# Edge network of a graph kernel: eight buffers for gathered source rows instead of four, loops of two iterations a turn, and weighted one-hots made in one vector instruction each

## What is computed

```python
h = relu(layernorm(x))                              # [12500, 96]
# edge network (the stage that is changed)
e = concat([h[src], edge_attr_32])                  # [400000, 128]
messages = gelu(e @ mW1 + mb1) @ mW2 + mb2
gates = sigmoid(gelu(e @ gW1 + gb1) @ gW2 + gb2)    # [400000, 1]
agg = segment_sum(messages * gates, dst, 12500)
update = gelu(concat([h, agg]) @ uW1 + ub1) @ uW2 + ub2
x = x + layernorm(h + update) * ln_g + ln_b
# two convolutions
h = relu(layernorm(x)); y = h
for W, b, Wr, br in layers:                         # 2 layers
    norm = dinv[src] * edge_weight * dinv[dst]      # self loops added
    conv = segment_sum(norm * (y @ W)[src], dst) + b
    g = sigmoid(y @ Wr + br)
    y = relu((1 - g) * y + g * conv)
out = x + y
```

## Time and profile before

| | |
|---|---|
| median of 3 runs | 11252.27 us (11244.29 to 11253.65) |
| the profiled execution | 11244.56 us, span 11242.6 us |
| edge pass, plain iterations (without building) | 160 to 680 us |
| edge pass, building iterations (175) | 680 to 5405 us |
| update stage | 5405 to 5650 us |
| the two convolution passes | 5650 to 11242 us |
| PE, PEld busy over the span | 8235.0 us (73%), 5614.5 us (50%) |
| DVE, ACT, POOL busy over the span | 5197.6 us (46%), 2896.6 us (26%), 6709.2 us (60%) |
| mean granted TensorE clock | 0.848 |

### The profile page before, as it was taken

How to read it: one execution, slowest core, us unless ns; L and a number is a source line. 1 busy time by engine, 2 the same in 40 slices (tenths; PEclk the granted TensorE clock), 3 DMA queues, 4 the chain that set the end, 5 groups by cost and what they waited for, 6 DMA issues and landing times.

```text
span 11242.6 us, 161615 instructions
## 1 busy us (share of the span) xinstructions
PE 8235.0 (73%) x40104; PEld 5614.5 (50%) x40104; DVE 5197.6 (46%) x17514; ACT 2896.6 (26%) x6502; POOL 6709.2 (60%) x6696
## 2 busy tenths in 40 slices
PE   5567666666767676667748888888875888888886
PEld 4334444444444444444435556555553555555554
DVE  5566666666666676666612222222231222222223
ACT  4345555555555555555300000000000000000000
POOL 4666565565566565656456666666645666666663
PEclk7678888888888888888768888888876988888887
DMA  4346566565566665656346666666664666666666
GB/s 151 81 132 175 166 175 172 167 174 168 171 174 175 172 176 172 172 168 174 128 144 230 229 236 237 228 232 233 228 205 152 232 225 235 231 233 232 232 229 204
DMA packets 1329034, 2149.88 MB, mean 191 GB/s; under 512 B 306427, under 2 KB 1079948, under 8 KB 1328700
## 3 DMA queue, kind: packets, MB, share of 16 engines
q10 hardware_dynamic: 142400, 986.64, 24.3%
q1 hardware_dynamic: 925996, 684.95, 20.7%
q0 software_dynamic: 260560, 477.49, 15.9%
HBM read 1587.45 MB, written 560.99 MB: 191 GB/s over the span
## 4 chain that ended last, share of the span: by engine, by line
PE 56%; issue 15%; another core or an unknown queue 15%; ACT 7%; DVE 3%; DMA 2%; POOL 1%; DVEq 1%; ACTq 1%; SPq 0%; POOLq 0%
PE bd L1159 30%; PE bd L1055 11%; PE sg L1146 6%; ACT blocks L1286 3%; PE pb L1044 3%; PE sg L1074 2%; PE pa L1044 2%; ACT hid L1265 2%; ACT msg L1278 1%; ACT gate_t L1271 1%; PE bd L1108 1%; PE bd L1171 0%; PE bd L1167 0%; DMA out_nodes<-s_c 0%
## 5 line engine op out<-in xcount | busy, mean ns | idle before, releaser
L909 POOL DMA_INDIRECT hid<-src_table,src_ids x3127 | 3188.8, 1020 | 2068.0 <-ACT msg L1278 1080.4
L1159 PE MATMUL bd<-ring,table_sb 128*96 128x280 f32 x13720 | 3580.3, 420 | 254.6 <-issue 145.1
L1159 PEld LDWEIGHTS bd<-ring,table_sb 128*96 128x96 f32 x13720 | 2332.5, 172 | 1408.7 <-issue 545.7
L1055 PE MATMUL bd<-one_hot_dst,one_hot_src 128*128 128x343 bf16 x8400 | 1751.2, 353 | 1449.9 <-ACT blocks L1286 1135.8
L953 POOL DMA_INDIRECT hid<-conv_table,hid x1724 | 1660.3, 963 | 1058.5 <-issue 512.4
L1055 PEld LDWEIGHTS bd<-one_hot_dst,one_hot_src 128*128 128x128 bf16 x8400 | 841.3, 108 | 2251.8 <-issue 1787.4
L1286 ACT ACTIVATE blocks<-bd 128x686 f32<-128x686 f32 x1400 | 1116.8, 798 | 2255.3 <-remote 1489.7
L953 POOL DMA_INDIRECT feat_in<-conv_table,hid x1152 | 1121.3, 973 | 618.3 <-issue 334.0
L1871 DVE TENSOR_TENSOR acc<-acc,sg 96x64 f32 x434 | 94.6, 218 | 2527.3 <-remote 1188.3
L1391 ACT ACTIVATE side_out<-bd,side_flag 96x280 f32<-96x280 f32 x70 | 34.3, 490 | 4022.5 <-issue 2294.1
L1885 DVE TENSOR_TENSOR acc<-acc,side_out 96x7 f32 x2800 | 469.6, 168 | 1256.2 <-issue 933.5
(11 more groups left out here) (226 smaller groups left out, 6957.8 us busy)
## 6 DMA issues: line engine op xcount, KB each, us to landing
ring<-adjacency ACTq DMA_DIRECT2D x980, 980.0 KB
adjacency<-blocks SPq DMA_DIRECT2D x700, 686.0 KB
attr<-in_attr SPq DMA_DIRECT2D x392, 128.0 KB
hid<-src_table,src_ids POOLq DMA_INDIRECT x3127
hid<-conv_table,hid POOLq DMA_INDIRECT x1724
feat_in<-conv_table,hid POOLq DMA_INDIRECT x1152
conv_table<-table_sb SPq DMA_DIRECT2D x28, 336.0 KB, 4.7
feat_half<-feat_keep SPq DMA_DIRECT2D x56, 168.0 KB
```

The source lines that it names most:

```text
L909: pool.indirect_dma_start(out=hid[s][:, t, :], out_offset=None, in_=src_rows, in_offset=bass.IndirectOffsetOnAxis(ap=src_ids[s // 2][:, j: ...
L1055: op = nc.tensor.matmul(bd[:, 512 * h:512 * h + HALF_Z], y[:, 1 + k, :], z[:, Z_PAD * h:Z_PAD * h + HALF_Z], start=(k == 0), stop=(k == 2))
L1159: op = nc.tensor.matmul(side_ps, table_sb[:, D * k:D * (k + 1)], ring[slot][:, :, QUAD_FANS * b:QUAD_FANS * (b + 1)], start=(k == 0), stop ...
```

## The change

It does three things.

**Eight buffers.** `hid` gets four more buffers, so that the quads of odd iterations have their own. They lie in memory that is free during the edge pass (`feat_space[0]`, `feat_space[1]`, `buf_h[1]`, `buf_b[1]`). Each has its own semaphore for landed gathers. POOL now starts quad s of iteration n when quad s of iteration n-2 has been weighed. The index lists keep their two buffers, and SP's program keeps its order: the list of a group is loaded after the gathers of that group of iteration n-1 have landed, and behind the store of four built tiles.

**Two iterations a turn.** Since a buffer's name must stand in the code, the loops over building iterations do two iterations a turn; the first two building iterations stand alone. ACT's early loads for the update stage that used the new buffers move behind its edge pass.

**One-hots.** The unweighted one-hot is gone. Each of the three weighted ones is made by one instruction that compares and multiplies (`is_equal`, then `mult`). That takes eight instructions of DVE out of each building iteration (L1601, 1400 in all) together with the wait between them and L1608, and leaves 24 instructions that now do two operations.

```diff
-            y_s = [sb_in(edges_phase, f"one_hot_src{i}", [P, 4, P], BF16) for i in range(SLOTS)]
+            y_s = [sb_in(edges_phase, f"one_hot_src{i}", [P, 3, P], BF16) for i in range(SLOTS)]
...
-        hid = [hid_all[:, QUAD * H2 * s:QUAD * H2 * (s + 1)].rearrange("p (t f) -> p t f", f=H2)
-               for s in range(QUADS_PER_ITER)]
+        hid_own = [hid_all[:, QUAD * H2 * s:QUAD * H2 * (s + 1)] for s in range(QUADS_PER_ITER)]
+        hid_own += [t[:, 0:QUAD * H2] for t in (feat_space[0], feat_space[1], buf_h[1], buf_b[1])]
+        hid = [t.rearrange("p (t f) -> p t f", f=H2) for t in hid_own]
...
-                with eng.Fori(alone, OCTETS - 1) as o:
-                    it = eng.snap(o + BUILD_FROM)
-                    iteration(it, n0 + it, False, False, (o, eng.snap(o0 + o)))
+                with eng.Fori(0, (OCTETS - 1 - alone) // 2) as v:
+                    for w in range(2):
+                        first = BUILD_FROM + alone + w
+                        it, turn = eng.snap(v * 2 + first), eng.snap(v + first // 2)
+                        o = eng.snap(v * 2 + (alone + w))
+                        iteration((it, turn, first % 2), n0 + it, False, False, (o, eng.snap(o0 + o)))
...
+        def slot_of(at, s):
+
+            it, turn, parity = at
+            return QUADS_PER_ITER * parity + s
...
-                            wait_apart(sp, s_gath[s], gathered(it - 1, QUAD, QUAD_SPARED[s]))
+                            slot = slot_of(before(at), s)
+                            wait_apart(sp, s_gath[slot], gathered(before(at)[1], slot))
                     sp.dma_start(src_ids[b][:, :], chunk(io["src"], it * 2 + b)).then_inc(s_ids[b], 16)
...
-                        wait_apart(pool, s_gated, QUADS_PER_ITER * (n - 1) + s + 1)
+                        wait_apart(pool, s_gated, QUADS_PER_ITER * (n - 2) + (s + 1 + GATED_CREDIT))
...
-                            out=hid[s][:, t, :], out_offset=None, in_=src_rows,
+                            out=hid[slot][:, t, :], out_offset=None, in_=src_rows,
...
-                for t in (t0, t0 + 1):
-                    v.tensor_scalar(y_s[t % SLOTS][:, 0, :], iota_lo[:, :], side_now[:, 0, t:t + 1], None,
-                                    ALU.is_equal).then_inc(s_one, 1)
-                for t in (t0, t0 + 1):
                     y, z = y_s[t % SLOTS], z_s[t % SLOTS]
                     v.tensor_scalar(z[:, :], iota_z[:, :], side_now[:, 4, t:t + 1], None, ALU.is_equal)
-                    dve.wait_ge(s_one, nb * OCTET + (t + 1))
                     for k in range(3):
-                        op = v.tensor_scalar(y[:, 1 + k, :], y[:, 0, :], side_now[:, 1 + k, t:t + 1], None, ALU.mult)
+                        op = v.tensor_scalar(y[:, k, :], iota_lo[:, :], side_now[:, 0, t:t + 1],
+                                             side_now[:, 1 + k, t:t + 1], ALU.is_equal, ALU.mult)
                     op.then_inc(s_yz, 1)
```

114 lines of the change are left out of this document (65 added, 49 removed).

## The result

| | before | after |
|---|---|---|
| median | 11248.6 us (4 runs) | 11995.9 us (4 runs, 11936.4 to 12042.1) |
| ratio | | 1.0646, 95% interval 1.0608 to 1.0684 |
| the profiled execution | 11244.6 us | 11951.6 us, span 11948.5 us |
| first to last block copy (175 iterations) | 674.3 to 5405.5 us | 714.0 to 6126.8 us |
| mean granted clock | 0.848 | 0.819 |

I had predicted 11450 us, and at most 11870. Slower was right; the size is 747 us instead of 200.

The account below looks back on a forecast made before the run. No engine full; a chain of waits sets the pace, with PE's results seen late during POOL's gathers. 11244.6 + 315 (buffers) - 120 (one-hots) + 4 (loads) = 11443.6, with 7.7 to the median 11450 us; range 10780 to 11870.

Parts of the forecast that it names:

- the reading that engines learn late of PE's results: Building iterations: while POOL gathers without pause, PE's results are seen only after the run; ACT waits 8.6 us an iteration.
- the 1000 us of POOL's waits: Building iterations: the most that more buffers could remove, 5.7 us of POOL's buffer waits in each of 175.
- the next limit: Building iterations: two index lists, loaded behind stores that wait for ACT's copies, limit POOL's lead to about six quads.
- its signs: POOL's pauses end with `src_ids`, SP waits for copies, ACT's remote waits stay at 8 us or grow, runs of 16 appear.
- The first rival: Building iterations: POOL's waits go and nothing replaces them, 21.4 to 22.5 us each, about 10350 us; chance 0.14.
- the buffers', +315 us: Building iterations: eight buffers bring no gain from POOL's side, 28.9 us each, +1.8 us; between 0 and +560 us.
- Its upper bound: Building iterations: 16 gathers on one list pause, 21.4 + 8.9 = 30.3 us an iteration.
- The pause for a list: POOL's pause in building: late results 1.44, copy 0.85, store issue 1.01, list 4.8, start about 0.8; together 8.9 us.
- The lower end: Building iterations: lists come in time and POOL's pauses stay as they are, 27.1 us an iteration.
- The last rival: Building iterations: each run held up fully, pause over 8.9 us for four quads; over 31 us, 12000 us; chance 0.05.
- The one-hots: DVE in building iterations: eight fewer instructions, two fifths of 1.76 us counted, -120 us, between 0 and -308; rows stay 258 ns.
- The update stage's loads: Start of the update stage: a DMA from ACT comes before PE's first product, 3 to 5 us once, +4 us.

Follow-up runs that it names:

- before_rest_again: Kernel before with only a small POOL power operation before each quad: 11258 us, ratio 1.0009 with late results; first run, before_rest, without them 10313 us, 1.1221.
- rest_one: lists_ahead plus a small POOL power operation before each quad, as a pause: 11274 us, ratio 0.9751 with late results; run again without them 10281 us, 1.1185.
- rest_two: lists_ahead plus a small POOL power operation before each second quad, after eight gathers: 11394 us, ratio 0.9851.
- pairs: lists_ahead, but POOL waits for two quads at once and starts eight gathers together: 9016 us, ratio 0.9821, on a chip without late results.
- the plain loads: Kernel before with ordinary DMAs of the same size from a fixed place instead of gathers: ratio 0.9438 (8663 us), again 0.8342 (9644 us).
- one_hots_alone: Kernel before with the new one-instruction one-hots and nothing else: 11533 us, ratio 1.0027.
- lists_ahead: Changed kernel with four index-list buffers, each list loaded an iteration earlier: 11530 us, ratio 1.0030.
- lists_old_hots: Eight buffers and four index lists loaded ahead as in lists_ahead, but one-hots made as before: 11595 us, ratio 1.0027.
- buffers_alone: Changed kernel with the one-hots made as before: 12146 us, ratio 1.0545.

## Why the prediction was wrong in size

**Right**: the reading that engines learn late of PE's results while POOL gathers without a pause. I had it as an inference. The rests show it: after every four gathers they take ACT's "remote" waits from 1268.1 to 121.7 us (before_rest_again) and to 226.9 (rest_one), after every eight they leave them at 1221.5 (rest_two). From it followed that eight buffers would not give the 1000 us of POOL's waits, and that was so: 1.0030 with the lists ahead. Right too was the next limit, with its signs: POOL's waits end mostly with `src_ids`, SP waits for copies alone, remote waits grow, more runs of 16 appear. The first rival (10350 us) is false on such a chip. On a chip without late results pairs reaches 20.2 us an iteration, as the rival said for POOL, yet gains only 1.8% on the kernel before, which takes 9184 us there and has no profile from that chip.

**Too strong**: that engines learn of the results when the run of gathers has ended. The copy of 3017.79 above starts with three gathers of the run still to come. Of the 270 copies with a "remote" wait in 1000 to 5000 us, 75, with 493 of the 1548 us, start when POOL has gathered for 3.5 us without a pause and goes on; in the kernel before it is 90 of 322, with 259 of the 1268 us. A run's end lets most results through, not all wait for it.

**The term that failed is the buffers', +315 us.** Its upper bound was 30.3 us an iteration and I took 28.9, "somewhat over the middle". Measured were 31.0, with the one-hots in it: +3.9 us instead of +1.8, 682 us instead of 315. The parts:

- The pause for a list: I had 8.9 us once an iteration, measured are 8.3 (131 waits in 128.9 iterations), and 11.19 in the one shown: 2.8 until the copy where I had 1.44, 2.0 for copy and store (1.86), 1.4 for the list's issue (nothing), 5.0 until POOL starts (5.6). In sum my pieces were about right.
- POOL's waits for messages: the bound put them at nothing, and 2.2 us an iteration are left.
- Gathers and the gaps between them: 20.5 us instead of 21.4.

So a list's pause came in nearly every iteration in full, and taking some half of it was the mistake: 1.4 of the 2.1 us an iteration that 28.9 us lacks. The other 0.7 us, some 120 us in all, the bound itself lacks, since it had no waits for messages; with the plain iterations below and the median, 44 us above the profiled execution and not 7.7, that puts the time above 11870 us. The lower end, "the lists come in time", needed copies in time, and by my own reading runs of gathers make copies late. It was no bound of the same mechanism but its denial, which was already counted as a rival.

The last rival, "much slower", had the time nearly right (over 31 us, 12000 us) at a chance of 0.05. Its single pause longer than 8.9 us is in the mean two waits, 8.3 us for lists and 2.2 us for messages.

**The one-hots**, -120 us, bounds 0 to -308, are the second step that failed. Measured: no gain; alone they cost 0.27%, some 30 us. By the means a row takes 322 ns, not 258; since DVE's instructions overlap a little, the busy times say better what is saved. Before, 259.8 + 683.0 us in 147.5 iterations are 6.39 us; after, 809.0/128.9 are 6.28 us. So 0.11 us of DVE's time were saved instead of 1.76: a second operation costs nearly what the dropped instructions gave back. I had ruled out a loss without a row that says so. The Trainium skill ("VectorE: DVE Perf Modes", Mode 4x_2P) has the second operation on compute slices of its own. That it would cost no time here was my conclusion, and this trace disagrees with that: 64 ns more for each of these instructions of 128 columns with two scalars. In which mode they ran no run shows.

**The plain iterations** were left out of the sum, as having no stores. They grew by 40 us in all: 24.6 to 26.1 us each (480 us for 294 gathers). Copies don't hold SP there, and still POOL now waits for lists, 75.0 us in 160 to 640 us. In SP's program the list also stands behind the load of the group before (L691), which waits for PE's attribute product, and that result comes late too. SP's waits for it with an unnamed end are 22.0 us before (L664, 160 to 640 us), and after:

```profile
SPq L691 <- remote: 147.9, 10, 21.3
```

So lists come late without any store too, and more lead is not free there either.

**The update stage's loads**: +4 us estimated; PE's first product waits 3.70 us for them, where it had waited 1.04 us, for the block copy. Yet what follows the last copy is 15 us shorter in all; where that is saved was not followed up:

```profile
6130.47 1.81 PE L1122 MATMUL pb<-feat_in,upd_top 96*96 96x448 f32 x2 [3.70 <-DMA feat_in<-feat_src]
```

**The rule of the Trainium skill** that PE and ACT wait on nobody ("SBUF — State Buffer", Who interferes with whom) was weighed against the copy of 3032.90. On chips where results come late the rows stay against it as far as it is taken to cover PE's signals; on the others the trace agrees (214.3 us of waits in pairs, all ended by PE). It speaks of memory ports, and no run here places the delay in one.

## What to carry to other kernels

Before giving a producer more buffers, list every input that it needs to start and see which of them stands in a queue behind the slow consumer: here the index list stood behind a store, and more lead only moved POOL's waits to the place where one wait costs most. A lead pays once; it raises the rate only if the producer is the limit. If waits end when another engine pauses, measure that effect alone (here with rests), see what else the experiment changes (the plain loads took the runs away too), and run it on more than one chip. And when a bound has been built from measured pieces, don't halve it toward an end that contradicts the mechanism it is built on.

## What was not expected of the hardware

- Results of PE come late during gathers in four of the six sessions (three chips of five). The kernel before takes 9184 and 9194 us on two chips, and 22 to 26% more in the other sessions. What makes the difference isn't known. It is not confined to the edge pass: before_rest and before_rest_again have the same iteration, 26.9 us, and differ by 918 us behind the last block copy (4911 and 5829 us).
- The delay needs a run of gathers: with 1.8 us of rest after every four the "remote" waits go from 8.6 to 0.8 us an iteration (121.7/148), with such a rest after every eight (rest_two) they stay at 8.5.
- A one-instruction compare-and-multiply of 128 bf16 columns takes 322 ns, the multiply alone 258. Yet gathers take 970 ns in one_hots_alone and 1022 before, 967 to 980 in lists_ahead and 1001 to 1025 in lists_old_hots; in buffers_alone, with the old ones, 983 to 990. The form of DVE's instruction may thus have given POOL something; it was not isolated.
- A list issued right behind a store of 2 x 686 KB reached POOL 5.0 us after its issue.
